# Linear attention in four chunks of 128 tokens instead of two of 256, in a decoder layer on one core

## The reference

```
qkv = silu(hidden_states @ qkv_w.T)
def step(kv, blk):                       # blocks of 64 tokens, one after the other
    scores = einsum('bhnd,bhmd->bhnm', cq, ck) * diag_decay
    intra  = einsum('bhnm,bhmd->bhnd', scores, cv)
    inter  = einsum('bhnd,bhde->bhne', cq * q_decay, kv)
    kv_next = kv * block_decay + einsum('bhnd,bhne->bhde', ck * k_decay, cv)
    return kv_next, intra + inter
xf = xf * rsqrt(mean(xf * xf) + EPS)     # over all heads, then norm_w
out = (sigmoid(hidden_states @ gate_w.T) * normed) @ out_w.T
```

## Time and profile before

| | |
|---|---|
| median of 3 runs (lowest, highest) | 1838.8 us (1838.69, 1839.65) |
| the profiled execution | 1839.74 us |
| its span | 1837.9 us |
| mean granted TensorE clock | 0.993 |
| DMA, mean over the span | 88 GB/s |

### The profile page before, as it was taken

One profiled execution on the slowest core, in us unless ns is written; L12 is line 12 of the kernel. 1 busy time (PEld: TensorE's weight loads), 2 busy tenths in 40 slices (PEclk: granted clock), 3 DMA queues, 4 the chain that ended last, 5 costly groups with the idle time before them and its releaser, 6 DMA issues.

```text
span 1837.9 us, 27416 instructions
## 1 busy us (share of the span) xinstructions
PE 1767.7 (96%) x9865; PEld 893.7 (49%) x9865; DVE 1336.3 (73%) x1867; ACT 971.3 (53%) x1432; POOL 639.8 (35%) x506
## 2 busy tenths in 40 slices
PE   6999999999999999999999999999999999999887
PEld 4454545445454545445454545445454545574333
DVE  7567776767777776767777767767677766659877
ACT  5565554655465554655464544555464544534674
POOL 2353333324333333324333333424333332302433
PEclk9999999999999999999999999999999999999998
DMA  4223224241423324141422214131322214133432
GB/s 174 86 69 104 75 92 109 69 109 47 136 66 103 75 92 109 69 110 46 135 67 70 75 58 110 58 86 47 99 68 69 76 58 109 58 107 124 115 93 92
DMA packets 158116, 161.52 MB, mean 88 GB/s; under 512 B 99872, under 2 KB 127904, under 8 KB 157600
## 3 DMA queue, kind: packets, MB, share of 16 engines
q1 hardware_dynamic: 146528, 147.09, 27.4%
q0 software_dynamic: 2560, 8.39, 1.4%
q10 hardware_dynamic: 8896, 4.28, 0.8%
HBM read 123.56 MB, written 12.58 MB: 74 GB/s over the span
## 4 chain that ended last, share of the span: by engine, by line
PE 85%; DVE 8%; issue 4%; ACT 2%; POOL 1%; DMA 0%; ACTq 0%; DVEq 0%; POOLq 0%
PE bank L1391 20%; PE bank L1393 20%; PE bank L1392 20%; PE bank L1364 7%; PE bank L1478 4%; PE bank L1479 4%; PE bank L1480 4%; DVE w_pair L1743 2%; DVE acc L1912 1%; PE bank L1446 1%; PE bank L1444 1%; PE bank L1445 1%; PE bank L1553 1%; PE bank L1542 1%; DVE x_blocks L1743 1%
## 5 line engine op out<-in xcount | busy, mean ns | idle before, releaser
L1391 PE MATMUL bank<-x_blocks,w_pair 128*128 128x512 f16 (+1 forms) x1820 | 677.9, 372 | 5.3 <-issue 1.7
L1393 PE MATMUL bank<-x_blocks,w_pair 128*128 128x512 f16 (+1 forms) x1820 | 677.9, 372 | 0.0
L1392 PE MATMUL bank<-x_blocks,w_pair 128*128 128x512 f16 (+1 forms) x1820 | 677.9, 372 | 0.0
L2030 POOL TENSOR_TENSOR sums_pair<-raw_pair 128x512 f32<-128x512 f32 x63 | 86.0, 1366 | 559.4 <-DVE w_pair L1743 404.9
L1391 PEld LDWEIGHTS bank<-x_blocks,w_pair 128*128 128x128 f16 x1820 | 178.0, 98 | 204.9 <-DVE bank L1791 4.8
L1393 PEld LDWEIGHTS bank<-x_blocks,w_pair 128*128 128x128 f16 x1820 | 178.1, 98 | 202.8
L1392 PEld LDWEIGHTS bank<-x_blocks,w_pair 128*128 128x128 f16 x1820 | 178.1, 98 | 188.3
L1912 DVE TENSOR_TENSOR acc<-acc,bank 128x512 f32<-128x512 f32 x320 | 210.5, 682 | 36.4 <-PE bank L1480 36.4
L1641 ACT ACTIVATE bank<-bank 128x512 f32<-128x512 f32 x145 | 84.7, 584 | 210.2 <-PE bank L1393 210.0
L2056 POOL TENSOR_TENSOR ssq<-ssq,sig 128x512 f32<-128x512 f32 x64 | 81.8, 1278 | 273.4 <-ACT sig L1662 273.4
L1743 DVE SCALAR_TENSOR_TENSOR w_pair<-raw_pair,w_pair 128x1024 f16<-128x1024 f32 x126 | 158.9, 1271 | 21.2 <-ACT w_pair L1606 21.1
(11 more groups left out here) (216 smaller groups left out, 2678.2 us busy)
## 6 DMA issues: line engine op xcount, KB each, us to landing
raw_pair<-w_qk SPq DMA_DIRECT2D x32, 1024.0 KB, 5.5
raw_pair<-w_gate SPq DMA_DIRECT2D x16, 1024.0 KB, 5.0
raw_pair<-w_out SPq DMA_DIRECT2D x16, 1024.0 KB, 4.9
raw_pair<-w_vt SPq DMA_DIRECT2D x15, 1024.0 KB, 4.9
raw_pair<-ctx_in SPq DMA_DIRECT2D x8, 1024.0 KB, 4.9
decay_sb<-rates SPq DMA_DIRECT2D x60, 128.0 KB, 4.9
acc<-x_t SPq DMA_DIRECT2D x4, 1024.0 KB, 11.3
ctx<-raw_pair SPq DMA_DIRECT2D x8, 512.0 KB, 3.1
```

The costliest lines, as they stand in the source:

```text
L1391: pe.matmul(out, w_hi, x_hi, start=unmet and k == 0, stop=False, skip_group_check=halves or not fresh)
L1392: pe.matmul(out, w_hi, x_lo, start=False, stop=False, skip_group_check=halves or not fresh)
L1393: mm = pe.matmul(out, w_lo, x_hi, start=False, stop=k == QT - 1, skip_group_check=halves or not fresh)
```

## The change

Attention of pairs 0 to 14 works in four chunks of 128 tokens. Inside a chunk there is one key tile, so `scores` and the values have four tiles of 128 columns, in one bank and one pass instead of two. Three states per head are needed: the first is a product of the first chunk, the second is the first times a constant (`CARRY`) plus the second chunk's product, the third is made from the second in the same way. ScalarE scales the first into `sig32`, VectorE adds, and multiplies and adds; ScalarE and VectorE split all three. All four blocks of k are decayed and turned (blocks 1 and 3 only their first tile, 128 tokens of each batch); the odd ones have a buffer of their own, `kd_late`, and land in the upper half of `decay_sb`. Rates and decays are loaded with 128 columns.

Reordered are: state(0) from slot "p1" ahead of the weight splits to "p7", attend(0) with scores(1) from "p7" to "p2", state(1) ahead of attend(1); in the q product unit 3's split and S2's right behind stage 0, and the SiLU of q's block 0 behind product 7; in the k product the turns and decays of the added blocks.

```diff
-HALF_GROUPS = ((0, 2), (1, 3))
+CHUNK_GROUPS = ((0, 1, 2, 3),)
+CARRY = [math.exp(-P * slope) for slope in SLOPES]
...
-        if which == "k" and r % 2 == 0:
-            self.kd[r // 2] = place, silu
+        if which == "k":
+            self.kd[r] = place, silu
...
+        free = self.late_kd_free if r % 2 else self.s_free
+        self.add("k_turn", r=r, gi=gi, rate=rate, free=free, hi=self.tick("kd_hi"), before=self.q_read)
...
         product_pair(plan, "gate", n, {
-            "p1": [state(0), part(0), part(1)] + [part(2), wo_sum],
-            "p7": [attend(0), score(1), gated(0)],
-            "p6": units(0) + [attend(1), gated(1), score(2), state(1)],
+            "p1": [part(0), part(1)] + [part(2), wo_sum],
+            "p7": [state(0)],
+            "p2": [attend(0), score(1), gated(0)],
+            "p6": units(0) + [state(1), attend(1), gated(1), score(2)],
...
-            "p2": sums(S2) + stages(0) + [lambda: plan.qk_out("q", 0)] + units(3),
-            "p7": split_sum(S2) + sums(S1) + sums(S4),
+            "p2": sums(S2) + stages(0) + units(3) + split_sum(S2),
+            "p7": [lambda: plan.qk_out("q", 0)] + sums(S1) + sums(S4),
...
-            "p5": stages(10) + [part(2)] + [turn(0)],
-            "p4": [decay(1)] + stages(11),
-            "p3": [part(0)],
+            "p5": stages(10) + [part(2)] + [turn(0), decay(3)],
+            "p4": [turn(3), decay(2)] + stages(11),
+            "p3": [part(0), turn(2), decay(1)],
...
# TensorE, attend and state
-                state = [c.k_t[:, st["h"] % GH, n, b, 0] for n in range(2)]
-                three(pe, c.banks[st["bank2"]][:, 0:HT], [(state, (q[:, 0], q[:, 1]))]).then_inc(sem["inter_mm"])
+                for k in range(1, NC):
+                    state = c.keys_of(st["h"] % GH, k - 1)
+                    mm = three(pe, c.banks[st["bank2"]][:, at], [((state[:, 0, b], state[:, 1, b]),
+                               (q[:, 0, k * P:(k + 1) * P], q[:, 1, k * P:(k + 1) * P]))], k == 1)
...
+            for k in range(2):
+                for b in range(B):
+                    mm = chunk(c.banks[st["bank"]][:, at:at + HD], k, b, at == 0)
+            mm.then_inc(sem["state_mm"])
+            for b in range(B):
+                mm = chunk(c.banks[st["bank2"]][:, b * HD:(b + 1) * HD], 2, b, b == 0)
             mm.then_inc(sem["state_mm"])
...
# ScalarE, state
-            act.activation(c.k_t[:, st["g"], 0, :, 0], c.banks[st["bank"]][:, 0:B * HD]..., ACT.Copy)
+            act.activation(c.k_t[:, st["g"], 0, :, 0], first..., ACT.Copy)
+            act.activation(sig[:, 0:HT], first, ACT.Copy, scale=CARRY[st["h"]]).then_inc(sem["carry"])
+            act.wait_ge(sem["carried"], st["second"][1])
+            act.activation(c.k_t[:, st["g"], 0, :, 1], sig[:, HT:S]..., ACT.Copy)
+            act.wait_ge(sem["carried"], st["third"][1])
+            act.activation(c.k_t3[st["g"]][:, 0], c.banks[st["bank2"]][:, 0:HT]..., ACT.Copy).then_inc(sem["st_hi"])
...
# VectorE, state
+            dve.tensor_tensor(sig[:, HT:S], sig[:, 0:HT], bank[:, HT:S], ALU.add).then_inc(sem["carried"])
+            dve.wait_ge(sem["state_mm"], st["mm2"][1])
+            dve.scalar_tensor_tensor(out=third, in0=sig[:, HT:S], scalar=CARRY[st["h"]], in1=third, op0=ALU.mult,
+                                     op1=ALU.add).then_inc(sem["carried"])
             dve.wait_ge(sem["st_hi"], st["hi"][1])
+            for k, src in enumerate((bank[:, 0:HT], sig[:, HT:S])):
+                split_low(src..., 1.0, hi, lo)
+            split_low(third..., 1.0, hi, lo).then_inc(sem["st_lo"])
```

More of the change, by code:

```diff
@@ L354, in decay_keys, with turn_keys @@
         self.release(place, rate)
[L355 to L360, removed]
+        self.kd[r] = gi, rate
+    def turn_keys(self, r):
+        gi, rate = self.kd[r]
+        free = self.late_kd_free if r % 2 else self.s_free
+        self.add("k_turn", r=r, gi=gi, rate=rate, free=free, hi=self.tick("kd_hi"), before=self.q_read)
         lo = self.sig_free[gi] = self.tick("kd_lo")
@@ L362, in turn_keys @@
         self.steps[-1]["lo"] = lo
[L363 to L370, removed]
+        self.k_turned[r] = self.tick(f"k_turned{r}", 16)
+        if r % 2:
+            self.late_kd_free = self.k_turned[r]
+        else:
+            self.s_free = self.k_turned[r]
@@ new lines, in state @@
+    def state(self, n, g):
+        (i, bank, free), (i2, bank2, free2) = self.main_ring.take(), self.main_ring.take()
+        gi = self.sig_at % 2
+        self.sig_at += 1
+        self.add("state", h=n * GH + g, g=g, gi=gi, sig_free=self.sig_free[gi], carry=self.tick("carry"), bank=bank, free=free, bank2=bank2, free2=free2,
+                 turned=self.k_turned[2 * g:2 * g + 2], v=self.v_first[g], v2=self.v_second[g], mm=self.tick("state_mm"),
+                 mm2=self.tick("state_mm"), second=self.tick("carried"), third=self.tick("carried"), hi=self.tick("st_hi"))
+        self.st_done[g] = self.sig_free[gi] = self.tick("st_lo")
@@ L371, in state @@
         self.main_ring.give(i, self.st_done[g])
+        self.main_ring.give(i2, self.st_done[g])
+        self.part_written.discard(bank)
+        self.part_written.add(bank2)
     def kv_out(self, b, r):
@@ L441, in scores @@
                       s_free=self.s_free, decay=self.decay_ready[h % 2], parts=[], whole=whole)
[L442 removed]
+        for _ in (SCORE_GROUPS if whole else CHUNK_GROUPS):
             i, bank, free = self.main_ring.take()
@@ L506, in out_stage @@
             taken = [self.main_ring.take() for _ in range(3)]
+            whole = next(j for j, t in enumerate(taken) if t[1] not in self.part_written)
+            taken[1], taken[whole] = taken[whole], taken[1]
+            self.part_written -= {t[1] for t in taken}
             self.out_at = dict(ring=[t[0] for t in taken], banks=[t[1] for t in taken], free=[t[2] for t in taken], read={})
@@ L1860, in vector_program @@
         elif kind == "k_decay":
-            k, src = (t.rearrange("p (b s) -> p b s", b=B) for t in (c.sig32[st["gi"]][:, :], c.placed(st["place"])))
+            out, src, g = c.sig32[st["gi"]][:, :], c.placed(st["place"]), st["r"] // 2
+            if st["r"] % 2:
+                out = out[:, 0:HT].rearrange("p (b s) -> p b s", b=B)
+                src = src.rearrange("p (b s) -> p b s", b=B)[:, :, 0:P]
+                rate = c.rate(g, B)
+            else:
+                out, src = (t.rearrange("p (c s) -> p c s", c=2 * B) for t in (out, src))
+                rate = c.rate(g, 2 * B)
             dve.wait_ge(sem["silu"], st["silu"][1])
@@ L2126 @@
         "decay": decay,
-        "rates": rows(np.broadcast_to(rates[:, :, None, :], (2, H, P, HT))),
+        "rates": rows(np.broadcast_to(rates[:, :, None, :], (2, H, P, P))),
         "ident": np.eye(P, dtype=np.float32),
```

116 lines of the change are left out of this document (74 added, 42 removed), and 4 rows, old and new, of the table FIRST.

## The result

| | before | after |
|---|---|---|
| median of the runs, us | 1838.74 (4 runs, 1838.41 to 1839.65) | 1924.66 (4 runs, 1923.41 to 1928.33) |
| span of the profiled execution, us | 1837.9 | 1923.4 |
| mean granted clock | 0.993 | 0.987 |

The ratio is 1.0463, 95% interval 1.0447 to 1.0479: 86 us slower, where 29 were forecast and the range ended at 1892. The direction and the three places named in the prediction were right; the size was wrong by a factor of three.

What follows compares the result with a forecast made beforehand. TensorE, busy 96% of the span, was taken as the bound, so its columns and stops count. Terms -18 - 11 + 30 + 6 + 22 = +29 gave 1869 us, range 1824 to 1892.

Steps and rivals of the forecast that it cites:

- the three places named in the prediction: Stop of about 2 us before state matmuls, about 1.6 us at an out product; 1.4 us stop gone or halved.
- Columns: TensorE streams fewer columns per unit, 2.35 us in place of 2.66, over 60 units: -18 us.
- Rival 4: Weight loads bind 128-column matmuls at 98 ns each: +88 in place of -18, so 1930 us; chance 0.03.
- The stop in q: Out product's 1.57 us wait for S2's split goes, `u3` comes 0.7 us late: gain 0.8 a pair, -11 us.
- State(0): Gate product: state(0) behind the weight splits makes TensorE stand at attend(0), 2.2 us computed, 2.0 taken: +30 us.
- State(1): State(1) ahead of attend(1) delays scores(2) for attend(2), and q's seed: 0.4 us a pair, +6 us.
- The keys: k product: turn(2) waits for turn(0)'s DMA ahead of ScalarE's seeds, out product stands 1.6 us: +22 us.
- Throughput of the others: Added VectorE (+2.7 us a pair) and ScalarE (+1.5) work is hidden by idle time; 40 us without that cover.

Runs made afterwards that it cites:

- e4: Kernel before (two chunks) with only the q product's new slots: unit 3's split and S2's behind stage 0, SiLU of block 0 behind product 7; 1832.99 us, ratio 0.9966.
- e8: Two-chunk kernel with the new q order and q's block 0 output moved to the head of the list behind product 6; 1822.16 us, ratio 0.9879.
- e5: Kernel after (four chunks) with the gate and q lists of before, k keeping the lists of after; 1898.22 us, ratio 1.0321.
- e10: Kernel after with state(0) first, state(1) behind scores(2), turn(2) behind the out seed, and q's block 0 behind product 6; 1862.45 us, ratio 1.0127.
- e13: Kernel after with every list sorted: state(0) first, wo_sum behind attend(0), state(1) behind score(2), q's block 0, units, stage 11 and turn(2) moved; 1868.36 us, ratio 1.0135.
- e14: Two-chunk kernel before with only the change's q order, timed again in turn with before in three rounds; 1836.20 us, ratio 0.9968.
- e3: Kernel after with GpSimd's sums of the out weights (wo_sum) moved behind attend(0); 1931.94 us, ratio 1.0472.
- e6: Kernel after with state(1) put back behind scores(2), as before the change; 1927.55 us, ratio 1.0448.
- e1: Kernel after with state(0) put back ahead of the weight splits in p1 of the gate product, attend(0) staying in p2; 1897.04 us, ratio 1.0283.
- e2: Kernel after with turn(2) moved behind the out seed of stage 12 in the v product; 1928.42 us, ratio 1.0453.
- e12: Kernel after with 12 matmuls of 512 columns, result overwritten, issued ahead of attend(0)'s wait for the state; 1915.50 us, ratio 1.0415.

## Why the prediction was wrong

Per pair the prediction comes to +1.9 us, and the period grew by 5.7; 15 x 5.7 is the 86 us. (The 29 us added to the median of before give 1868; the forecast has 1869.) Two steps failed: the work of the other engines, which was put at nothing, and the price of the stop at attend(0), which was put too low. By the prediction's own steps:

- **Columns, -18: right.** 128-column matmuls stand 0.056 us apart in after too. Period less stops and clock is 101.2 us for the two-chunk kernels (before, e4, e8) and 99.9 for the four-chunk ones (after, e5, e10, e13): 1.2 us a pair forecast and 1.2 measured. Rival 4 (loads bind at 98 ns) is refuted. The Trainium skill ("TensorE: Matmul & The Clock Gate", section Back-to-back issue gap) has some 81 ns for such a pair of load and matmul; the trace does not agree in these runs of 12 and 21, where it is 56 ns.
- **The stop in q, -11: right in its places, and its size half.** 1.57 went, 0.81 at `u3` came (0.7 forecast). e4 and e14 measure it alone at -5 to -6 us, since another 0.28 us a pair came behind `u3`.
- **State(0), +30: the mechanism right, the cost wrong.** Its chain was right, and its computed 2.2 us are what e3 measured when GpSimd was elsewhere. I took 2.0 in place of the 2.2, and left out two things: GpSimd's adds beside the splits (+0.77) and the clock behind a 3 us stop (1.3 to 1.6 us in half the pairs). The 15 stops measured 44 us and the clock behind them 10, so 54 us, or 3.6 a pair, against 30 forecast and an upper end of 39.
- **State(1), +6:** 0.85 us at attend(2) and 0.19 at a product behind it, 15 us, the upper end. The cause I gave is not borne out (e6): the order of state and attention moves the stop and does not shorten it.
- **The keys, +22: right in its chain, a third too large.** ScalarE stands 2.44 us on the turn's DMA ahead of its seeds (2.5 forecast), and TensorE 1.30 us in the pair shown and 1.1 on average (1.6 forecast, 1.7 computed), 16 us. The rows of ACT and PE:

```profile
838.41 0.63 ACT L1714 ACTIVATE scores_keys<-sig 128x512 f16<-128x512 f32 x1 [2.44 <-DMA scores_keys<-scores_keys]
840.19 0.58 ACT L1669 ACTIVATE bank<-bank 128x512 f32<-128x512 f32 x1 [1.15 <-PE bank L1426]
840.68 0.58 ACT L1734 ACTIVATE bank<-bank 128x512 f32<-128x512 f32 x1
```

```profile
841.32 0.39 PE L1525 MATMUL bank<-w_vo,gated_split 128*128 128x512 f16 x1 [1.14 <-ACT bank L1734]
```

- **Throughput of the others, 0: wrong.** It was costed at nothing "between the chains", with 40 us named as its price without cover. Part of that came due at places that I had not walked through: product 7 of q waits for the gate of the third quarter (0.82), stage 12 for stage 11's add, which two more decays and turn splits push back (0.52; e13, which puts stage 11 ahead of them, has no such stop), and a product on `c22` (0.28). That is 1.6 us a pair, 24 us. The gate's place was taken away by no run (0.73 to 0.82 in e5, e10 and e13), so that the added work makes it late is read from the queues and not shown.

With the measured values: columns -1.2, q -0.8, attend(0) 3.0 and clock 0.65, attend(2) 1.0, out seed 1.1, the stop behind `u3` 0.3, the unpredicted ones 1.6: 5.7 us a pair, and the period grew by 5.7. Of the miss of 3.8 us a pair 1.6 are the work of the others, 1.6 the term of state(0), 0.6 attend(2), 0.3 the stop behind `u3` that the new order of q brings in e4 as well, less 0.4 of the keys.

The interaction is in the results as well: four chunks with the old gate and q lists +59, q's order alone -6, all together +86. The remaining 33 us agree with what e1 takes back by moving state(0) out of the place behind product 7 again; as stops pass on from place to place (e1, e3, e6), such terms need not add up in general.

What stays open: why the clock falls behind a 2.98 us stop in every second pair of after and in every pair of e2; and whether a four-chunk kernel can come under e8. Its columns would give 18 us, and its best orders here left 5.2 (e10) and 5.1 us (e13) of stops a pair, where e8 has 0.7.

## What to carry to other kernels

When TensorE is the bound and the other engines look a quarter to a half idle, cost every added instruction by the chain that it lengthens, at each place of the period where TensorE is released, and look at what GpSimd and the DMAs do in the same microseconds; a total of idle time hides nothing by itself. A stop of TensorE of 2 to 3 us cost more than its length here in part of the pairs, so it can pay to fill it (e12); breaking it into short ones was not timed by itself, but e5, whose stops are all shorter, had no slow stretch. When a change bundles a restructuring and a reordering, time each alone: here the reordering, taken one step further, was worth 1.2%, and the restructuring hid it.

## What the runs showed of the hardware

- A VectorE scalar_tensor_tensor from SBUF to SBUF took 1.19 us for 128x256 (0.41 to 0.43 otherwise) and 1.37 us for 128x512 (0.68 otherwise) while GpSimd ran 128x512 float32 adds; splits from PSUM of the same stretch kept their 0.41 to 0.43 us. The added time looks like a wait for the add that was under way: the split ends 0.28 us behind the end of that add (759.42 behind 759.14) or, at 512 columns, 0.54 behind it (in e1, 752.36 behind 751.82). Where the split began first it kept its 0.69 us, and the add took 1.65 us, against 1.27 while VectorE added from PSUM:

```profile
721.40 0.69 DVE L1798 SCALAR_TENSOR_TENSOR scores_keys<-sig,scores_keys 128x512 f16<-128x512 f32 x1
721.57 1.65 POOL L2104 TENSOR_TENSOR sums_pair<-raw_pair 128x512 f32<-128x512 f32 x1 [12.17 <-DVE w_pair L1798]
704.21 1.27 POOL L2104 TENSOR_TENSOR sums_pair<-raw_pair 128x512 f32<-128x512 f32 x1 [16.25 <-DMA raw_pair<-w_vt]
```

- Behind stops of TensorE of 2.1 to 3.2 us the granted clock went to the 1.2 GHz level for 3.4 us, in some pairs and not in others (6 of the 13 stops of 2.98 us in after, 13 of 13 in e2, 2 of the stops of 2.1 in e1), where the pairs of before have 1.00; with the stop filled it never did, and before, e4, e5, e8 and e13, whose repeated stops are 1.6 us or less, have no such stretch in their pairs.
- Matmuls of 128 columns, each with its own weight load, kept 0.056 us from start to start in runs of 12 and of 21, and those of 512 columns 0.216 us, at a granted clock of 1.00.
- Before took 1838.7, 1839.2, 1840.8, 1844.3 and 1844.8 us in the five sets of runs, which were made on at least four chips.
